# A scan and a routed expert layer in one kernel: sums, routing groups and weight loads re-timed

## The chip, the cores and the metric

The kernel runs on one core of a Trainium2 chip. Its engines are TensorE (PE in the profile, weight loads as PEld), VectorE (DVE), ScalarE (ACT), GpSimd (POOL) and SyncE (SP), which issues DMAs. Each has its own instruction stream; they wait for one another through semaphores. The metric is the time of one execution in microseconds.

## The reference, cut to what matters

The input x is 2 batches of 1024 tokens with 256 features. First comes a state-space layer: per batch 512 channels with 16 states each, `h = exp(delta*A)*h + delta*u*B` along the 1024 tokens, `y = sum over the 16 states of h*C`, then `(y + u*D) * silu(z)`, projected to 256 features by Wout and added to x. Then a layer norm, a router with 8 experts, and the experts:

```
gate_logits = x @ gate_kernel;  top 2 of 8, softmax over the two
h0 = x @ w0[e];  h1 = x @ w1[e];  inter = silu(h0) * h1        # 256 -> 512
out = sum over the two experts of weight * (inter @ wo[e])     # 512 -> 256
x = x + gb * out
```

All is float32.

## The kernel before, in words

**Scan stage.** The channels of the two batches make 8 chunks (batch times 4) of 128 partitions and 1024 tokens. Per chunk and state k of 16: TensorE spreads B into PSUM (`front`, L646), VectorE multiplies it into a drive (L1326; for states 2, 6, 10 and 14 ScalarE copies and GpSimd multiplies, L1034 and L1654), ScalarE makes the decay (L1028), VectorE scans (L1338), GpSimd multiplies with C (L1630, `weigh`), and TensorE adds the product to the chunk's sum in PSUM by an identity matmul (`back`, L664; the first of a chunk begins with u*D, L659). TensorE issues the spread of state k+4 at step k and then the sum of step k. In the last three chunks other work of TensorE takes the place of the sums in the first four steps (`pieces` of `blocks_behind`): outward matmuls of batch 0's tokens (`outward_y`), then turning of its normed tokens (`turned_in`, L701). The sums lag and are caught up, two at every other step. GpSimd may be at most six products ahead of the sums. With the last three sums go the logits of batch 0 in three pieces (`first_logits`, L720), and turning back the first two pairs of tiles (`turned_back`, L710) stands before the last sum. The ranks of batch 0 (`ranks`, L811) come after all that.

**Routing.** A token's row goes, with its position and weights, to a region of a scratch tensor in DRAM for each of its two experts. `pick`, `weights` and `place_of` on VectorE find the top two, the softmax and the destination; GpSimd sends the rows by indirect DMA, 128 rows each (`send`, L1677). The work goes in groups of token tiles, `GROUPS`: batch 0 (8 tiles, 16 sends), then two groups of 4 tiles (8 sends each). For batch 1 TensorE makes the outward matmuls (L686), VectorE adds and norms (`residual`, `normal_h2`), GpSimd takes the reciprocal root (`rstd_of`, L1659 and L1661) between its sends, TensorE turns and makes the logits (`scored`, L786 and L794). After the last group VectorE computes a table of which expert and which rows the later slots take (L1506 to L1532, end: semaphore `c_over`).

**Expert stage.** 39 slots of 128 rows: slots 0 to 7 are the first 128 rows of each expert, the others come from the table. SyncE loads a slot's rows (`rows_in`, L474). TensorE's order per slot is: turn the rows of the slot two ahead (L834), turn this slot's activations (L857), the hidden matmuls of the next slot (L849), the outward matmuls of this slot (L866). ScalarE copies and applies silu (L1147, L1153). VectorE: `take_inter` copies the turned activations (L1544), `noted_of` notes four numbers of a row, `gate_h` multiplies (L1539), `leave` weights the output (L1560, L1565). GpSimd adds each output into the result by an indirect DMA (L1714). There are two output buffers; `leave` of the first slots waits on `yo_free`, which GpSimd first raises after the last group's sends have landed (end of the GpSimd stream). Before slot 8 SyncE waits for `c_over`, for all sends, and for eight writes of zero rows behind the experts' rows, which ScalarE issues among its slots (`tail`, L1161; the wait is L494).

**Weights.** 512 KB per matrix, three per expert. SyncE loads the w1 of experts 4 to 6 during the last scans, all of experts 0 to 3 when the last sum is made, the others behind the row loads of slots 1 to 4. The hidden matmuls of an expert wait for the weights of its pair (0 and 1, 2 and 3, ...).

## Time and profile before

| | |
|---|---|
| median of 3 runs | 850.11 us (849.39 to 853.98) |
| profiled execution | 850.03 us, span 848.2 us |
| PE busy | 737.5 us (87%), 2292 instructions |
| DVE busy | 626.6 us (74%) |
| POOL busy | 513.4 us (61%) |
| ACT busy | 340.2 us (40%) |
| HBM | 98.08 MB read, 24.69 MB written |
| chain that ended last | PE 30%, of it L849 16% and L866 8% |
| queue q8, instructions | 12 packets, 0.20 MB |

The profile is of one execution. Busy times are those of an engine's instructions. The chain of waits is followed back from the last instruction to what released each step. The strip of 40 slices, each 21.2 us, shows the stages (busy tenths):

```
PE   5799998888797887878989878986699999999994
DVE  4478889999899998999999898846444444444442
POOL 1013233999999999999999898947522222222222
PEclk9999999999999999999999987997599999999998
```

### The profile page before, as it was taken

To read this page: it belongs to the slowest core of one execution; us is meant where nothing else is said; L and a number is where in the kernel's file an instruction comes from. 1 tells how busy PE (TensorE), PEld (TensorE's weight loads), DVE (VectorE), ACT (ScalarE), POOL (GpSimd) and SP (SyncE) were. 2 spreads that over 40 slices of the span, in tenths; PEclk is the share of its full clock that TensorE was granted. 3 is DMA by queue.
4 is the path that set the end of the run, shared out by engine and by line. 5 is a ranking of instruction groups with operands and counts; after the bars stand their busy time and mean duration, and the time that the engine had idled before them with its cause. 6 is when DMAs were issued, how large, how long until landed. Compare 5 with 4: busy or idle time off the path is not lost. (4 is left out here: it accounts for less than half of the span.)

```text
span 848.2 us, 9598 instructions
## 1 busy us (share of the span) xinstructions
PE 737.5 (87%) x2292; PEld 370.5 (44%) x2293; DVE 626.6 (74%) x840; ACT 340.2 (40%) x387; POOL 513.4 (61%) x271
## 2 busy tenths in 40 slices
PE   5799998888797887878989878986699999999994
PEld 2444343233232332324535323465366666666663
DVE  4478889999899998999999898846444444444442
ACT  0776966456453543545445475311111111111110
POOL 1013233999999999999999898947522222222222
PEclk9999999999999999999999987997599999999998
DMA  9354645866667666676759968567662322222220
GB/s 282 98 158 148 186 158 148 205 183 175 174 158 195 176 175 181 175 188 168 207 159 238 231 138 244 143 238 244 202 203 45 49 45 34 49 46 38 46 30 0
DMA packets 62296, 126.41 MB, mean 149 GB/s; under 512 B 11898, under 2 KB 33850, under 8 KB 62140
## 3 DMA queue, kind: packets, MB, share of 16 engines
q1 hardware_dynamic: 50468, 116.12, 50.0%
q0 software_dynamic: 7152, 8.48, 5.7%
q10 hardware_dynamic: 4648, 1.48, 0.7%
q8 instruction: 12, 0.20, 0.1%
q14 instruction: 16, 0.13, 0.1%
HBM read 98.08 MB, written 24.69 MB: 145 GB/s over the span
## 5 line engine op out<-in xcount | busy, mean ns | idle before, releaser
L1630 POOL TENSOR_TENSOR pool<-pool,hT 128x1024 f32<-128x1024 f32 x101 | 235.8, 2355 | 15.8 <-PE PS L664 15.8
L664 PE MATMUL PS<-pool,ident 128*128 128x512 f32 x404 | 206.3, 637 | 31.0 <-POOL pool L1630 30.2
L1028 ACT ACTIVATE PS<-pool,negA 128x1024 f32<-128x1024 f32 x128 | 143.1, 1118 | 168.3 <-DVE pool L1338 168.3
L1714 POOL DMA_INDIRECT out<-uT,ptab x39 | 60.6, 1555 | 169.1 <-DVE uT L1565 157.9
L1338 DVE TENSOR_TENSOR_SCAN pool<-PS,pool 128x1024 f32<-128x1024 f32 x64 | 143.0, 2270 | 3.4 <-ACT PS L1028 3.4
L849 PE MATMUL PS<-pool,uT 128*128 (+1 forms) x312 | 145.3, 610 | 0.0
L664 PEld LDWEIGHTS PS<-pool,ident 128*128 128x128 f32 x404 | 75.8, 198 | 118.4 <-issue 59.3
L646 PE MATMUL PS<-pool 96*128 96x512 bf16 x256 | 80.8, 398 | 27.9 <-DVE wz_sb L1326 12.0
L1539 DVE TENSOR_TENSOR uT<-uT,PS 128x512 f32<-128x512 f32 x39 | 26.9, 689 | 88.4 <-PE PS L849 85.6
L1654 POOL TENSOR_TENSOR spread<-spread,pool 128x1024 f32<-128x1024 f32 x32 | 75.4, 2355 | 15.3 <-ACT spread L1034 15.3
L849 PEld LDWEIGHTS PS<-pool,uT 128*128 128x128 f32 x312 | 58.3, 197 | 59.0 <-issue 59.0
L1326 DVE TENSOR_TENSOR pool<-PS,pool 128x1024 f32<-128x1024 f32 x64 | 76.9, 1202 | 8.9 <-PE PS L646 8.9
L1338 DVE TENSOR_TENSOR_SCAN pool<-PS,spread 128x1024 f32<-128x1024 f32 x32 | 73.0, 2282 | 8.2 <-POOL spread L1654 6.4
L866 PE MATMUL PS<-Y,uT 128*128 (+1 forms) x312 | 73.8, 379 | 0.9 <-DVE uT L1544 0.9
L1338 DVE TENSOR_TENSOR_SCAN pool<-PS,wz_sb 128x1024 f32<-128x1024 f32 x32 | 72.9, 2277 | 0.0
L646 PEld LDWEIGHTS PS<-pool 96*128 96x128 bf16 x256 | 22.0, 101 | 112.8 <-DVE pool L1326 35.5
L866 PEld LDWEIGHTS PS<-Y,uT 128*128 128x128 f32 x312 | 59.2, 190 | 25.3 <-issue 19.3
L1630 POOL TENSOR_TENSOR Y<-pool,hT 128x1024 f32<-128x1024 f32 x27 | 63.2, 2356 | 3.5 <-PE PS L664 3.5
L1147 ACT ACTIVATE uT<-PS 128x256 f32<-128x256 f32 x39 | 15.0, 385 | 121.1 <-PE PS L834 121.1
L664 PE MATMUL PS<-Y,ident 128*128 128x512 f32 x108 | 53.2, 622 | 1.8 <-POOL Y L1630 1.3
L559 PE MATMUL PS<-hT,pool 128*128 x112 | 50.6, 598 | 3.1 <-DVE Y L1281 2.4
L1153 ACT ACTIVATE uT<-PS 128x512 f32<-128x512 f32 x39 | 23.3, 598 | 74.3 <-PE PS L849 72.5
(197 smaller groups left out, 867.3 us busy)
## 6 DMA issues: line engine op xcount, KB each, us to landing
hT<-C_scratch SPq DMA_DIRECT2D x128, 512.0 KB, 5.3
pool<-in_w SPq DMA_DIRECT2D x16, 512.0 KB
uT<-expert_in_scratch SPq DMA_DIRECT2D x39, 130.5 KB
Y<-Y SPq DMA_DIRECT2D x32, 128.0 KB, 2.4
C_scratch<-Y SPq DMA_DIRECT2D x8, 512.0 KB, 2.6
pool<-du_scratch SPq DMA_DIRECT2D x8, 512.0 KB, 6.1
Y<-in_wo SPq DMA_DIRECT2D x8, 512.0 KB
expert_in_scratch<-zrow SPq DMA_DIRECT2D x16, 130.5 KB, 5.8
```

Source lines behind the costliest of these rows:

```text
L559: m = pe.matmul(PS[:, bank + half, :], w(k), rhs(k, half), start=k == 0, stop=k == k_chunks - 1)
L646: m = pe.matmul(PS[:, 4 + half, :], sel[0:PARTS * 32, k, :], stk[0:PARTS * 32, r, HF * half:HF * half + HF], start=True, stop=True)
L664: m = pe.matmul(PS[:, 6 + half, :], ident[:, :], prod_k[:, HF * half:HF * half + HF], start=False, stop=k == DS - 1)
L849: m = pe.matmul(PS[:, bank, :], xgT[:, r, k, :], w[:, bass.ds(e, 1), k, :].rearrange("p e n -> p (e n)"), start=k == 0, stop=k == KD - 1)
L866: m = pe.matmul(PS[:, 6 + r, 0:DM], intT[:, r, k, :], wo_sb[:, bass.ds(e, 1), k, :].rearrange("p e n -> p (e n)"), start=k == 0, stop=k == ...
L1028: act.activation(pair(2 * (k % 2)).unsqueeze(1), delta[:, chunk_at(g2, r), :], ACT.Exp, scale=decay[:, bass.ds(g2 * (2 * DS) + n, 1)]).the ...
L1326: dve.tensor_tensor(dbu_of[owned_to(k) % 3], pair(4), du[:, r, :], ALU.mult).then_inc(dbu_done, 1)
L1338: dve.tensor_tensor_scan(hst[:, k % HR, :], pair(2 * (k % 2)), driven, 0.0, ALU.mult, ALU.add).then_inc(scan_done, 1)
L1539: dve.tensor_tensor(inter[:, r, :], sil[:, r, :], PS[:, 3 + 2 * r, :], ALU.mult).then_inc(inter_done, 1)
L1630: gp.tensor_tensor(to, hst[:, k % HR, :], crep[k % RC], ALU.mult).then_inc(prod_done, 1)
L1654: gp.tensor_tensor(spread[:, :], spread[:, :], du[:, r, :], ALU.mult).then_inc(shared_done, 1)
L1714: gp.indirect_dma_start(out=out, out_offset=bass.IndirectOffsetOnAxis(ap=ptab[:, slot:slot + 1], axis=0), in_=yo[:, slot % 2, :], in_offse ...
```

## The change

Six edits. (1) The lagging sums: a table `CATCH_UP` says at which steps two are made, and the four `turned_in` go as two pairs in the first two steps of the last chunk, so that its sums begin at step 2 and not 4; ScalarE takes them as two pairs too. (2) The logits of batch 0 are one piece before sum 12; its ranks stand before sum 14, and all turning back stands behind the last sum, ScalarE's copies of it behind the copy of the sums. (3) Batch 1 is one group of 8 tiles with 16 sends, picked after both halves are normed. (4) GpSimd's sends of batch 0 are cut 10, 5, 1 around the two `rstd_of` instead of 7, 6, 3. (5) The table is cut in three parts, which VectorE computes after the outputs of slots 0, 1 and 2; the zero rows move from ScalarE's iterations 0 to 3 to 2 to 5. (6) Weights: expert 0 at the last sum, experts 1 and 2 with the first six outward tiles of batch 1, the others behind the row loads of slots 2 to 6.

```diff
-GROUPS = ((0, NTB), (NTB, NTB + TQ), (NTB + TQ, NT))
+GROUPS = ((0, NTB), (NTB, NT))
@@ SyncE
-            for e in range(CH):
-                w0_of(e)
-                w1_of(e)
-                wo_of(e)
-            sp.wait_ge(gated, NG)
-            x2_stored(slice(NTB, NTB + TQ))
+            w0_of(0)
+            w1_of(0)
+            wo_of(0)
+            for t in range(NTB, NT):
+                sp.wait_ge(o_mm, t + 1)
+                if t - NTB < 6:
+                    (w0_of, w1_of, wo_of)[(t - NTB) % 3](1 + (t - NTB) // 3)
+                if t == NTB + 6:
+                    x2_stored(slice(NTB, NTB + TQ))
...
-                if e in (1, 2, 3, 4):
-                    w0_of(e + 3)
-                    if e == 4:
-                        w1_of(e + 3)
-                    wo_of(e + 3)
+                if 2 <= e < NE - 1:
+                    w0_of(e + 1)
+                    if e + 1 < CH or e + 1 == NE - 1:
+                        w1_of(e + 1)
+                    wo_of(e + 1)
@@ TensorE
+            CATCH_UP = {0: (), 2: (4, 6), TQ: (6, 8, 10, 11)}
...
             def blocks_behind(g2, r, pieces, last):
-                made = 0
+                made, behind = 0, len(pieces)
+                sums_at = [0] * behind + [1] * (DS - behind)
+                for k in CATCH_UP[behind]:
+                    sums_at[k] += 1
                 for k in range(DS):
                     next_front(g2, r, k, last)
-                    if k < len(pieces):
-                        pieces[k]()
-                        continue
-                    for _ in range(min(2 - (k - len(pieces)) % 2, k + 1 - made)):
-                        if last and made >= DS - 3:
-                            first_logits(range(3 * (made - DS + 3), min(3 * (made - DS + 3) + 3, NTB)))
-                        if last and made == DS - 1:
-                            turned_back(0)
-                            turned_back(1)
+                    if k < behind:
+                        pieces[k]()
+                    if last and k == DS - LAG:
+                        first_logits()
+                    for _ in range(sums_at[k]):
                         if made == 0:
                             pair_read(2 * g2 + r)
+                        if last and made == DS - 2:
+                            ranks(0)
                         back(g2, r, made, prod_at(DS * (2 * g2 + r) + made))
                         made += 1
...
-            blocks_behind(NB + 1, 1, [lambda j=j: turned_in(j) for j in range(NTB // 2)], True)
-            turned_back(2)
-            turned_back(3)
+            blocks_behind(NB + 1, 1, [lambda i=i: turned_pair(i) for i in range(2)], True)
+            for j in range(NTB // 2):
+                turned_back(j)
...
-            ranks(0)
@@ ScalarE
-                if g == CH + 3 and k in range(LAG, LAG + NTB // 2):
-                    take_turned(k - LAG)
+                if g == CH + 3 and k in (LAG, LAG + 1):
+                    take_turned(2 * (k - LAG))
+                    take_turned(2 * (k - LAG) + 1)
...
-            take_rows2(0)
-            take_rows2(1)
             gap_exp(0)
             leave(NG // 2 - 1, 1)
-            take_rows2(2)
-            take_rows2(3)
+            for j in range(NTB // 2):
+                take_rows2(j)
...
-            act.wait_ge(known, 2)
-            for s2 in range(2):
+            for s2 in range(NE // 2):
                 for r in range(2):
                     take_rows(s2 + 1, r)
                     silu_h(s2 + r, 1 - r)
-                    tail(4 * s2 + 2 * r)
-                    tail(4 * s2 + 2 * r + 1)
+                    if s2 in (1, 2):
+                        if s2 == 1 and r == 0:
+                            act.wait_ge(known, 2)
+                        tail(4 * (s2 - 1) + 2 * r)
+                        tail(4 * (s2 - 1) + 2 * r + 1)
@@ VectorE
-            residual(1)
-            normal_h2(1)
-            residual(2)
+            residual(NTB, NTB + TQ)
+            normal_h2(NTB, NTB + TQ)
+            residual(NTB + TQ, NT)
+            normal_h2(NTB + TQ, NT)
             pick(1)
             weights(1)
             place_of(1)
-            normal_h2(2)
-            pick(2)
-            weights(2)
-            place_of(2)
...
-            dve.wait_ge(c_over, 1)
             dve.wait_ge(regated, 1)
...
+            def slots_of(s2, between):
                 for r in range(2):
                     take_inter(s2, r)
                     noted_of(s2 + 1, r)
                     gate_h(s2 + r, 1 - r)
                     leave(s2, r)
+                    if between:
+                        between.pop(0)()
+
+            between = [count_slots, expert_of_slots, rows_of_slots]
+            slots_of(0, between)
+            slots_of(1, between)
@@ GpSimd
-            send(0, slice(0, 7))
+            send(0, slice(0, 10))
             rstd_of(2)
-            send(0, slice(7, 13))
+            send(0, slice(10, 15))
             rstd_of(3)
-            send(0, slice(13, 16))
+            send(0, slice(15, 16))
...
             for q in range(1, NQ):
                 gp.wait_ge(placed, q + 1)
-                send(q, slice(0, 2 * TQ))
+                send(q, slice(0, 2 * NTB))
```

`count_slots`, `expert_of_slots` and `rows_of_slots` hold the instructions of the old table, L1508 to L1532, in their order. `turned_pair(i)` calls `turned_in(2 * i)` and `turned_in(2 * i + 1)`.

## Rows read from the trace of the kernel before

**Rows 1.** Busy PE, PEld, DVE, ACT, POOL by stretch; clock, DMA, GB/s.
```profile
610.20:619.00 8.80, 8.76 (x22) 5.22 (x23) 2.23 (x7) 0.98 (x2) 0.80 (x1) 0.66 1.02 355
...
619.00:833.70 214.70, 214.70 (x812) 134.53 (x811) 100.03 (x292) 36.01 (x73) 57.54 (x37) 1.00 0.28 51
```

**Rows 2.** The chain that ended last: start us, duration us, what.
```profile
558.06 1.10 PE PS L811 x44
...
585.93 2.59 DMA expert_in_scratch<-pool,posu
...
607.25 2.95 DMA uT<-expert_in_scratch
...
611.78 5.67 PE PS L849 x8
...
617.45 1.73 PE PS L866 x8
...
619.83 3.44 PE PS L849 x8
...
623.27 1.73 PE PS L866 x8
```

**Rows 3.** TensorE in order of time: start, duration, line, operation, count, idle before.
```profile
516.65 3.78 PE L659 MATMUL PS<-uT,ident 128*128 128x512 f32 x4 [0.43 <-ACT uT L1095]
...
555.30 1.88 PE L664 MATMUL PS<-pool,ident 128*128 128x512 f32 x4
```

**Rows 4.** The same view of VectorE and GpSimd, last chunk.
```profile
522.46 2.34 POOL L1630 TENSOR_TENSOR Y<-pool,hT 128x1024 f32<-128x1024 f32 x1 [3.55 <-PE PS L664]
...
524.47 1.23 DVE L1326 TENSOR_TENSOR pool<-PS,pool 128x1024 f32<-128x1024 f32 x1 [3.83 <-PE PS L646]
...
547.87 4.64 POOL L1630 TENSOR_TENSOR pool<-pool,hT 128x1024 f32<-128x1024 f32 x2
```

**Rows 5.** The same view of ScalarE and TensorE after the sums.
```profile
558.23 1.08 ACT L1100 ACTIVATE pool<-PS 128x512 f32<-128x512 f32 x2
...
562.12 15.45 PE L686 MATMUL PS<-wout_sb,uT 128*128 128x256 f32 x64 [2.97 <-DVE uT L1471]
```

**Rows 6.** The same view of GpSimd, the sends.
```profile
561.64 1.43 POOL L1677 DMA_INDIRECT expert_in_scratch<-pool,posu  x1 [8.81 <-DVEq L1467]
...
572.65 1.13 POOL L1661 TENSOR_TENSOR rstd<-rstd,nhalf 128x4 f32<-128x4 f32 x1
...
600.95 0.96 POOL L1677 DMA_INDIRECT expert_in_scratch<-pool,posu  x1 [2.63 <-DVEq L1467]
...
610.03 0.96 POOL L1677 DMA_INDIRECT expert_in_scratch<-pool,posu  x1 [0.30 <-issue]
```

**Rows 7.** The same view of VectorE, the router.
```profile
554.58 0.22 DVE L1411 COPY spread<-PS 128x64 f32<-128x64 f32 x1 [5.86 <-PE PS L720]
...
557.14 0.23 DVE L1425 TENSOR_TENSOR spread<-spread 128x64 bf16<-128x64 f32 x1
...
588.99 1.67 DVE L1402 SCALAR_TENSOR_TENSOR pool<-hT,rstd,grow 128x256 f32<-128x256 f32 x4
...
594.94 0.19 DVE L1411 COPY spread<-PS 128x32 f32<-128x32 f32 x1 [4.29 <-PE PS L794]
...
599.59 0.19 DVE L1452 TENSOR_TENSOR spread<-PS,e_rows 128x32 f32<-128x32 f32 x1 [1.80 <-remote]
```

**Rows 8.** The same view of VectorE, first output of the slots.
```profile
619.38 0.48 DVE L1565 SCALAR_TENSOR_TENSOR uT<-PS,wtab,uT 128x256 f32<-128x256 f32 x1 [0.81 <-DVE uT L1560]
```

**Rows 9.** The same view of TensorE, ScalarE, SyncE; and the wait of L494.
```profile
630.65 0.38 PE L834 MATMUL PS<-ident,uT 128*128 128x128 f32 x2
...
633.90 1.54 ACTq L1161 DMA_DIRECT2D expert_in_scratch<-zrow  x2
...
L494 SPq EVENT_SEMAPHORE  x1: 4061/4061/4061, 633.7 to 633.7; - x1
...
638.96 17.47 SPq L474 DMA_DIRECT2D uT<-expert_in_scratch  x4
```

More of the change, by code:

```diff
@@ L722, in first_logits, with ranks @@
                     m.then_inc(g_mm, 1)
+            def ranks(q):
+                first, end = GROUPS[q]
+                n = end - first
+                pe.wait_ge(tables, 1)
+                pe.wait_ge(picked, q + 1)
+                for i in range(n + (q in (0, NQ - 1))):
+                    to = PS[:, r_bank(q), P + NE * i:P + NE * i + NE]
+                    parts = [(ones[:, :], ohs[:, first + j, :]) for j in range(i)]
+                    if q:
+                        parts.append((ones[:, :], sums[:, q, :]))
+                    if i < n:
+                        parts.append((tri[:, :], ohs[:, first + i, :]))
+                    for j, (w, rhs) in enumerate(parts):
+                        m = pe.matmul(to, w, rhs, start=j == 0, stop=j == len(parts) - 1)
+                m.then_inc(rank_mm, 1)
             def next_front(g2, r, k, last):
@@ L796, in logits @@
                 m.then_inc(g_mm, 1)
-            def ranks(q):
-                first, end = GROUPS[q]
-                n = end - first
-                pe.wait_ge(tables, 1)
-                pe.wait_ge(picked, q + 1)
-                for i in range(n + (q in (0, NQ - 1))):
-                    to = PS[:, r_bank(q), P + NE * i:P + NE * i + NE]
-                    parts = [(ones[:, :], ohs[:, first + j, :]) for j in range(i)]
-                    if q:
-                        parts.append((ones[:, :], sums[:, q, :]))
-                    if i < n:
-                        parts.append((tri[:, :], ohs[:, first + i, :]))
-                    for j, (w, rhs) in enumerate(parts):
-                        m = pe.matmul(to, w, rhs, start=j == 0, stop=j == len(parts) - 1)
-                m.then_inc(rank_mm, 1)
             def scored(q):
@@ L1471, in gate_y, with residual @@
                 dve.tensor_tensor(uT[:, c, :], uT[:, c, :], szT[:, c, :], ALU.mult).then_inc(gated, 1)
-            def residual(q):
-                first, end = GROUPS[q]
+            def residual(first, end):
                 added_y(first)
@@ L1481, in residual, with normal_h2 @@
                     gathered(t)
-            def normal_h2(q):
-                for t in range(*GROUPS[q]):
+            def normal_h2(first, end):
+                for t in range(first, end):
                     centre(t)
-                for t in range(*GROUPS[q]):
+                for t in range(first, end):
                     h2_of(t)
@@ L1575, in _ @@
             gate_h(0, 0)
-            with dve.Fori(0, SPAIRS) as s2:
+            def slots_of(s2, between):
                 for r in range(2):
```

76 lines of the change are left out of this document (42 added, 34 removed).

## The prediction

> **What bounds the kernel now.** I read the page's strip of 40 slices first (PE at 9 of 10 from slice 32 on), then the chain of waits, and from there each engine in order of time. Three stages follow one another. From 620 us on a slot of the expert layer costs the same 5.82 us each time (617.45 to 623.27 in [rows 2]), TensorE is busy 214.70 of 214.70 us at a granted clock of 1.00, its 2.4 GHz level [rows 1]; half clock below is its 1.2 GHz level, and 39 slots end near 834 us. An edit moves the end only by moving the start of this stream or by opening a gap in it. Before it the scans end, GpSimd finishes its products at 552.5 [rows 4], TensorE its sums at 557.2 [rows 3]. Between them lies routing (557 to 600), a chain through all engines.
>
> Below, iteration j of the expert stream means: turn the rows of slot j+2, turn slot j's activations, hidden matmuls of slot j+1, outward matmuls of slot j. Iteration 0 starts at 610.24, iteration 3 at 630.65 [rows 9].
>
> **Sums of the last chunk.** Before, the first sum waits for ScalarE's copies of the turned tiles, starts at 516.65 at half clock [rows 3], and is done with its identity matmul when GpSimd resumes (522.46, after 3.55 us idle) and VectorE gets its next drive (524.47, after 3.83) [rows 4]. Now both pairs of tiles are turned in steps 0 and 1 and the first sum stands at step 2, ahead of two spreads of B that used to precede it. The ACT copies end near 513.6, so the first sum ends near 519.1, but VectorE's drive of state 7 is behind it and the scan that GpSimd's product 6 needs ends near 523.1. GpSimd has no gap after that before and is the bound to product 15, so its end moves +0.7, last product 553.2. Bounds: if TensorE stays at half clock through the first sum +2.2; if it runs at full clock throughout -1.5. I take +0.7, because the rows around it show half clock. The other re-timed sums (steps 6, 8, 10, 11) trade one 0.46 us stall for another: 0.
>
> The logits now go in one piece before sum 12, while GpSimd is still multiplying, and the router of batch 0 on VectorE starts when the last scan ends (about 550) instead of 554.58 [rows 7]. Ranks stand before sum 14. The tables are free early, but the last sum still waits for product 15: 555.30 + 1.8 becomes about 557.5 at its end. Turning back all four pairs (16 transposes, 1.8 us) now follows it, and ScalarE copies them after the sum's own copy. Four halves of 0.54 [rows 5] behind a 1.0 us copy end at 561.1, where before they ended at 559.3. The outward matmuls, which also waited for the gate that stood behind the router on VectorE, start at 561.2 instead of 562.12 [rows 5]: -0.9. The sends wait for the same copies: 561.6, as before (561.64) [rows 6].
>
> **Batch 1 as one group.** A send costs 1.30 us (600.95 to 610.03 is seven steps [rows 6]). Ten sends (13.1) put the first rstd at 574.7, where before it had to wait for its data until 572.2; its two operations [rows 6] end at 576.4. Five sends (6.6) and the second rstd (1.5) end at 584.6. The last four h2 rows follow at 584.8; before, the like group began at 588.99 and its last logits were read at 594.94 [rows 7], 5.9 us later. So 590.7. Picking eight tiles takes 2.8 to 2.9 (554.58 to 557.37 [rows 7]), against 1.9 for four. The ranks are 9*8/2 + 9 + 8 = 53 matmuls against 44 in 1.10 us at full clock [rows 2]; at half clock I take 1.9 (bounds 1.3 and 2.2). Places 1.3. So the places of batch 1 are known at 596.8, against 600.6 before: -3.8. I cost the 1.80 us that VectorE sat until a "remote" release at 599.59 [rows 7] at nothing in the new kernel, since the DMA engines are quiet then: weights of expert 3 and up are asked for only with slot 2.
> The Trainium skill (Runtime: NRT & Kernel Launch, section Instruction fetch mechanics) says that each sequencer refills its instructions in 16 KiB blocks by its own DMA, mostly hidden; the page's queue q8 with 12 packets and 0.20 MB agrees on the size, and the wait beside full DMA slices does not agree on "hidden". If such a refill still costs 1.8 us here, everything below is 1.8 later.
>
> **Into the slots.** The tables of later slots (VectorE 600.9 to 605) leave the path; slot 0's first turn comes at 595.7, its hidden matmuls at 597.3 (before 600.61), and the 3.4 us that TensorE waited for slot 2's rows (released by a 2.95 us transfer [rows 2] that had been issued behind the tables) go. Iteration 0 would end near 609.7 where before it ended at 619.0. The tables cost 1.2, 1.3 and 1.6 us behind the outputs of slots 0, 1 and 2, where VectorE has some 2.7 us before its next copy is missed: 0. The weights are 1.5 MB for expert 3 between slots 2 and 3, and at the 355 GB/s of [rows 1] they take 4.4 us, within one slot, while slot 2 is not multiplied before iteration 1: 0.
>
> **What is late next: the output buffers.** VectorE's output of slot 0 waits for a semaphore that GpSimd raises only behind all sends of batch 1. Before, eight sends stood behind the last places: 600.95 to 611.0, plus 1.6 us to landing (585.93 + 2.59 against an issue of 0.96 [rows 2, 6]), 612.6, and the output at 619.38 waited for nothing but its own engine [rows 8]. Now sixteen stand there. Placed at 596.8, first send at 597.2, last issued at 597.2 + 15*1.31 + 0.96 = 617.8, landed 619.4. The output of slot 0 is wanted at 609.7 and gets 619.5 to 620.0; behind it on VectorE stand the count of the slots (1.2) and the copy of slot 1's activations (0.7), so slot 1's outward matmuls start at 622.0. TensorE has then idled since about 613.5. Before, those matmuls started at 623.27 [rows 2]: -1.3. But they now start behind an idle time. Before, TensorE restarted at 610.24 after 3.4 us idle, and to 617.45 took 7.2 us for what costs 4.3 later (5.67 against 3.44 for the same eight matmuls [rows 2]): 2.9 us at half clock. The other such restart, 562.12, cost 1.7. I take 2.9: from iteration 2 on the stream stands at **+1.6**. Bounds -2.5 (places and sends 3 us earlier, restart at 1.7) to +4.5.
>
> **The tails, moved two iterations back.** ScalarE writes zero rows behind each expert's rows, two per iteration, formerly in iterations 0 to 3, now in 2 to 5. SyncE may load slot 8 only when all eight have landed. Before, iteration 3 started at 630.65, the last pair was issued from 633.90, SyncE's wait for them lasted 4.06 us from 633.7 to 637.8, and slot 8's load was issued at 638.96 [rows 9]. With 2.3 to 2.95 us to landing ([rows 2], a busier moment) its rows are there at 641.8, 11.2 us after the start of that iteration. That load is not used before iteration 6, so it cost nothing. Now the last pair is in iteration 5, its rows come 11.2 us after that starts, and TensorE wants them as the first thing of iteration 6, 5.82 after: a gap of **5.4 us** (4.6 to 6.5). Everything on TensorE stands behind that turn. The restart costs another 2.2 (between the two rows, 1.7 and 2.9). Slot 9's load is issued right after slot 8's, so the gap comes once.
> The Trainium skill (DMA: Bandwidth & Descriptors, section Anatomy of one DMA) fits a transfer as 2.0 us plus its bytes at 436 GB/s; 130.5 KB would be 2.3 us, near the short end of what I read for the load, and with it the gap would be 4.9.
>
> **Sum.** Stream +1.6, gap +5.4, restart +2.2: +9.2 on a span of 848.2. The profiled execution took 850.03, 1.8 more than its span, and stands at the median (850.11). So 859.2.
>
> **Rivals.**
> (a) *Only the buffers are late.* If slot 8's rows come in time, the stream's +1.6 is all: 851.7. For it: SyncE has slack everywhere else. Against it: the wait of 4.06 us is in the trace already, and only its three spare iterations hid it.
> (b) *Neither is late, faster.* The stream starts when slot 2's rows allow, 9.3 us earlier, ends 9.3 earlier: 840.8. It needs the 16 sends to be done before 609, when slot 0's output is wanted; it decides where sends plus landing take less than 12 us. Against it: 1.30 us each.
> (c) *Only the gap at slot 8.* -9.3 + 5.4 + 2.2 = -1.7: 848.3. It needs the same early sends.
> (d) *The scans starve.* TensorE at half clock through the last chunk keeps VectorE waiting for its drives and the sends start 3 us later; everything hangs on the sends, so 862.2, and to 866 where a refill is added.
> The spreading of the weights may not do what it says: at six of the steps SyncE waits for outward tiles that come every 1.7 us, as fast as 512 KB arrive, so the DMA engines stay as full as before until 577. That changes no term.
>
> **How the numbers follow.** Forecast 0.62; (a) 0.13; (b) 0.08; (c) 0.05; (d) 0.12. The forecast's own range is 853 to 864. For 8 in 10 I go from 850.5 to 864.5, which takes in (a) and most of (d). About 0.5% (4.3 us) is what a measurement of this kernel can tell from no change. Slower (over 854.4): 0.57 of the forecast and (d), together 0.69. Same: (a), (c) and the forecast's low end, 0.21. Faster: (b) and what is left, 0.10.
>
> **What would show it.** In the new trace: the first output of VectorE in the slots released by GpSimd's last sends, not by TensorE, near 619.5; TensorE idle some 8 us in iteration 1 before slot 1's outward matmuls, at half clock behind it; SyncE waiting several us for the zero rows after slot 7's load; TensorE idle about 5 us, once, before the turn of slot 8, near 649; and 5.82 us a slot afterwards. The forecast is wrong if the first output comes before 612, if slot 8's turn has no idle time before it, or if the places of batch 1 come later than 600.

## The result, and the profile after

The changed kernel took 864.89 us, median of 4 runs (857.29 to 866.55); the kernel before, beside it, 849.75, median of 4 (847.76 to 853.98). The ratio is 1.0154, 95% interval 1.0081 to 1.0227: slower, by somewhere between 0.8 and 2.3%. Run again on another chip it was 1.0145 (1.0098 to 1.0192). The profiled execution took 863.47 with a span of 861.7, 13.5 us more than the span before. The forecast was 859.2, so the direction was right. The profiled 863.47 lies in the forecast's own range (853 to 864), the median is 0.9 us above it and 0.4 above the range for 8 in 10. Of the 5.7 us between forecast and median, 4.3 are in the profiled execution and are to be explained; the other 1.4 are the distance of the median from it.

I follow the time from the front. VectorE in the last two chunks (start us, duration, what, and the idle time before it with its releaser):

```profile
495.41 1.22 DVE L1336 TENSOR_TENSOR pool<-PS,pool 128x1024 f32<-128x1024 f32 x1 [1.69 <-PE PS L651]
...
522.21 1.23 DVE L1336 TENSOR_TENSOR wz_sb<-PS,pool 128x1024 f32<-128x1024 f32 x1 [5.76 <-PE PS L651]
```

The second row answers to the 3.83 us of [rows 4]; the prediction had this drive behind the first sum and put +0.7 us on it for GpSimd. The first has no answer there: in the chunk before the last, where the plan of the sums has two at a time at steps 10 and 11, VectorE now waits for the spread of B, which TensorE makes behind them. TensorE, from step 11 of that chunk to the outward matmuls:

```profile
489.72 5.16 PE L669 MATMUL PS<-Y,ident 128*128 128x512 f32 x8
...
516.09 3.78 PE L664 MATMUL PS<-uT,ident 128*128 128x512 f32 x4 [2.94 <-ACT uT L1104]
...
548.02 4.53 PE L724 MATMUL PS<-gate_sb,uT 128*128 128x8 f32 x32 [0.63 <-DVE wz_sb L1336]
552.41 6.25 PE L669 MATMUL PS<-Y,ident 128*128 128x512 f32 x8
...
559.60 3.68 PE L669 MATMUL PS<-pool,ident 128*128 128x512 f32 x8
563.11 1.91 PE L715 MATMUL PS<-ident,uT 128*128 128x128 f32 x16
566.48 3.69 PE L691 MATMUL PS<-wout_sb,uT 128*128 128x256 f32 x16 [1.46 <-ACT pool L1109]
```

GpSimd's last product ends at 555.85. Before it ended at 552.5 and the last sum ran at 555.30 [rows 3, 4], behind two other pieces of TensorE's:

```profile
553.59 0.95 PE L720 MATMUL PS<-gate_sb,uT 128*128 128x8 f32 x8
554.40 1.07 PE L710 MATMUL PS<-ident,uT 128*128 128x128 f32 x8
```

Here the logits are one block of 4.53 us and the two sums behind it take 6.25 for x8 (3.68 for the like x8 at 559.60). TensorE is busy all the time, but at the 1.2 GHz level for about 6 us. By stretches, columns as in [rows 1], the changed kernel and then the kernel before:

```profile
551.00:557.00 6.00, 6.00 (x14) 3.42 (x14) 5.50 (x31) 0.21 (x1) 5.23 (x5) 0.50 0.01 1
```
```profile
550.00:553.00 3.00, 3.00 (x17) 2.10 (x16) 0.00 (x0) 0.00 (x0) 2.83 (x4) 1.00 0.00 0
```

What TensorE did before the clock fell were the 32 narrow matmuls of the logits (8 columns each) in one piece. All six traces that have them in one piece show the fall, for about 3 to 6 us; in the eight that have them in three pieces between sums the granted clock stays at 1.00 there. Then come the ranks, from 558.49 on, right behind the two sums, and two sums are still to do when they end. The last sum ends at 563.1, 7.2 us behind the last product; before it was 4.7.

GpSimd's sends of batch 1, its first row and its last, and the add into the output behind them:

```profile
602.71 1.06 POOL L1696 DMA_INDIRECT expert_in_scratch<-pool,posu  x1 [11.09 <-DVEq L1477]
...
621.83 0.96 POOL L1696 DMA_INDIRECT expert_in_scratch<-pool,posu  x1 [0.30 <-issue]
626.89 1.62 POOL L1733 DMA_INDIRECT out<-uT,ptab  x1 [4.10 <-DVE uT L1576]
```

Sixteen steps of 1.27 us, one behind the other, where [rows 6] had eight. The chain of waits runs through all sixteen, then through their landing:

```profile
621.83 3.50 DMA expert_in_scratch<-pool,posu
625.60 0.48 DVE uT L1576
627.04 0.70 DVE uT L1555
627.78 3.78 PE PS L875 x8
```

VectorE and TensorE there; the row of VectorE answers to [rows 8], where it waited for nothing but its own engine:

```profile
625.60 0.48 DVE L1576 SCALAR_TENSOR_TENSOR uT<-PS,wtab,uT 128x256 f32<-128x256 f32 x1 [11.99 <-POOLq L1727]
```
```profile
627.78 3.78 PE L875 MATMUL PS<-Y,uT 128*128 128x256 f32 x8 [7.19 <-DVE uT L1555]
```

The releaser is GpSimd's queue at L1727, the raise of the buffers' semaphore behind the sends. The outward matmuls take 3.78 for what takes 1.73 at the other clock level. The last gap, in the chain and in the view of TensorE:

```profile
652.71 0.34 ACTq L1169
...
653.83 2.63 DMA expert_in_scratch<-zrow
657.71 2.04 DMA uT<-expert_in_scratch
659.80 0.55 PE PS L843 x2
...
661.21 4.58 PE PS L858 x8
...
668.18 3.44 PE PS L858 x8
```
```profile
659.80 0.55 PE L843 MATMUL PS<-ident,uT 128*128 128x128 f32 x2 [4.36 <-DMA uT<-expert_in_scratch]
```

SyncE's longest wait for the zero rows (in total us, times, longest), 4.06 before in [rows 9]:

```profile
SPq L497 <- DMA expert_in_scratch<-zrow: 14.3, 1, 14.3
```

By stretches of 10 us, columns as in [rows 1], granted clock after the busy times:

```profile
610.00:620.00 10.00, 7.87 (x27) 4.33 (x26) 1.18 (x4) 0.94 (x2) 7.56 (x9) 1.00 1.04 356
620.00:630.00 10.00, 2.81 (x7) 1.85 (x6) 3.33 (x14) 0.64 (x2) 3.80 (x4) 0.79 0.46 141
630.00:640.00 10.00, 10.00 (x36) 6.63 (x35) 5.42 (x16) 1.37 (x3) 2.12 (x2) 0.87 0.84 234
640.00:650.00 10.00, 10.00 (x40) 6.42 (x39) 5.06 (x16) 1.70 (x4) 2.56 (x2) 1.00 0.68 191
650.00:660.00 10.00, 5.64 (x21) 3.17 (x20) 3.02 (x9) 0.86 (x2) 3.09 (x2) 1.00 0.33 63
660.00:670.00 10.00, 10.00 (x33) 6.04 (x32) 3.88 (x13) 1.44 (x4) 0.92 (x1) 0.83 0.12 32
```

TensorE loses 7.2 us in the second stretch and 4.4 in the fifth, and has the lower clock behind each. Hidden matmuls of iteration 2 begin at 632.6 against 625.5 before: +7.1. Those of iteration 7 begin at 668.18 against 654.74: +13.4, which is the whole difference of the spans. So 7.1 to 7.2 come from the start of the stream and 6.25 from slot 8.

### The profile page after: what moved, and what is told of

The parts are those of the page before. It is cut to its first block and busy times, and to the rows that moved or that the text cites. A ratio compares the mean times of both kernels' runs of the same rounds, so it can differ in the third digit from the quotient of the medians.

```text
span 861.7 us, 9562 instructions
## 1 busy us (share of the span) xinstructions
PE 738.7 (86%) x2312; PEld 371.3 (43%) x2313; DVE 624.0 (72%) x824; ACT 340.0 (39%) x386; POOL 512.6 (59%) x271
## 5 line engine op out<-in xcount | busy, mean ns | idle before, releaser
L1733 POOL DMA_INDIRECT out<-uT,ptab x39 | 60.6, 1555 | 170.8 <-DVE uT L1576 159.7
L858 PE MATMUL PS<-pool,uT 128*128 (+1 forms) x312 | 143.0, 602 | 0.0
L651 PE MATMUL PS<-pool 96*128 96x512 bf16 x256 | 78.4, 388 | 33.6 <-DVE pool L1336 15.4
L875 PE MATMUL PS<-Y,uT 128*128 (+1 forms) x312 | 75.7, 386 | 8.1 <-DVE uT L1555 8.1
```

What stands on the lines that cost most here:

```text
L651: m = pe.matmul(PS[:, 4 + half, :], sel[0:PARTS * 32, k, :], stk[0:PARTS * 32, r, HF * half:HF * half + HF], start=True, stop=True)
L858: m = pe.matmul(PS[:, bank, :], xgT[:, r, k, :], w[:, bass.ds(e, 1), k, :].rearrange("p e n -> p (e n)"), start=k == 0, stop=k == KD - 1)
L875: m = pe.matmul(PS[:, 6 + r, 0:DM], intT[:, r, k, :], wo_sb[:, bass.ds(e, 1), k, :].rearrange("p e n -> p (e n)"), start=k == 0, stop=k == ...
L1733: gp.indirect_dma_start(out=out, out_offset=bass.IndirectOffsetOnAxis(ap=ptab[:, slot:slot + 1], axis=0), in_=yo[:, slot % 2, :], in_offse ...
```

## The experiments

Beside the first two, the kernels ran in four sets, each on a chip of its own and at a time of its own, and the kernel before beside each. Its median there was 842.42 (set A), 849.09 (B), 844.76 (C) and 848.16 (D). The scans differ by up to 6 us between traces, so each kernel has two numbers: its ratio within its set, and, from its trace, the time **from the last product to the end** of the span. All in us; P: last product ends; then from P to the first send, to the end of the last send's issue, to the end of the span; then the waits of VectorE behind 540 us whose releaser the profile calls "remote", of which more below:

```
kernel                  set  median  ratio  [95%]             P       send  sends  end    "remote"
before                  -    849.75  -                        552.45   9.2   58.5  295.8  3.73, 1.80
before, again           D    847.72  1.000  [0.997, 1.003]    549.23   9.2   60.7  296.8  3.83, 1.82
changed                 -    864.89  1.0154 [1.0081, 1.0227]  555.85  11.6   64.4  305.9  -
changed, again          B    862.00  1.0145 [1.0098, 1.0192]  553.09  11.6   66.9  305.1  4.17
e1 zero rows 4 + 4      A    854.18  1.0117 [1.0070, 1.0165]  553.27  11.6   66.8  299.1  -
e2 buffers early        A    860.30  1.0191 [1.0133, 1.0250]  553.14  11.6   66.3  305.6  -
e3 three groups         A    850.99  1.0093 [1.0060, 1.0126]  553.11   9.9   55.0  295.6  -
e4 old logits           B    858.72  1.0105 [1.0076, 1.0135]  554.12   9.2   64.7  302.3  -
e5 old plan and logits  A    853.60  1.0131 [1.0076, 1.0187]  548.67   9.2   64.7  302.5  -
e6 before, tails late   B    854.50  1.0066 [1.0038, 1.0093]  550.97   9.2   58.7  300.1  3.8, 1.8
a2 changed, old weights C    865.26  1.0216 [1.0168, 1.0264]  558.52  11.6   61.8  305.0  -
c1 combined             B    845.01  0.9951 [0.9922, 0.9979]  554.59   9.2   60.6  293.9  1.89, 4.06
c1 combined, again      C    841.98  0.9968 [0.9939, 0.9996]  548.84   9.2   54.7  288.0  -
c2 combined, old weights C   843.85  0.9970 [0.9941, 0.9999]  554.30   9.2   54.6  288.1  -
```

**The two late things, each alone.** e1 takes the changed kernel and issues the zero rows four at a time in iterations 2 and 3, so that the last land two iterations earlier:

```diff
-                    if s2 in (1, 2):
-                        if s2 == 1 and r == 0:
+                    if s2 == 1:
+                        if r == 0:
                             act.wait_ge(known, 2)
-                        tail(4 * (s2 - 1) + 2 * r)
-                        tail(4 * (s2 - 1) + 2 * r + 1)
+                        for e in range(4 * r, 4 * r + 4):
+                            tail(e)
```

> The changed kernel with one edit: ScalarE issues its eight zero-row writes in iterations 2 and 3, four in each, and not two in each of iterations 2 to 5. My theory: the 4.4 us that TensorE idles before the turn of slot 8, and the restart at half clock behind it (together 6.2 us in the changed kernel), come from the last of these writes. Then both go: 6.2 us faster than the changed kernel (864.9), about 858.7. A rival (slot 8's rows are late for another reason, the later table or the sends that must have landed): no change, 864.9.

VectorE's wait for the buffers stays, 11.21 us (TensorE waits 8.3), and the gap at slot 8 is gone: the hidden matmuls of iterations 5 and 6 start at 647.2 and 653.0, 5.8 apart. From the last product to the end it is 299.1, 6.0 less than the changed kernel's own second trace (305.1) and 6.8 less than its first, as the theory said. By the ratios alone (1.0117 against 1.0145 and 1.0154) it would be 2 to 3 us; the last experiments tell why ratios of different sets don't compare. The row of VectorE:

```profile
622.24 0.48 DVE L1576 SCALAR_TENSOR_TENSOR uT<-PS,wtab,uT 128x256 f32<-128x256 f32 x1 [11.21 <-POOLq L1727]
```

e6 does the reverse: the kernel before, with nothing but its zero rows in iterations 2 to 5.

```diff
-            act.wait_ge(known, 2)
-            for s2 in range(2):
+            for s2 in range(NE // 2):
                 for r in range(2):
                     take_rows(s2 + 1, r)
                     silu_h(s2 + r, 1 - r)
-                    tail(4 * s2 + 2 * r)
-                    tail(4 * s2 + 2 * r + 1)
+                    if s2 in (1, 2):
+                        if s2 == 1 and r == 0:
+                            act.wait_ge(known, 2)
+                        tail(4 * (s2 - 1) + 2 * r)
+                        tail(4 * (s2 - 1) + 2 * r + 1)
```

> The kernel before with one edit: ScalarE's zero rows two iterations later, as in the change. My theory: TensorE idles 4.4 us before the turn of slot 8 and restarts at half clock: 6.2 us slower than before, ratio 1.0074. A rival (the gap in the change needs its other edits, the later weight loads above all): no change, 1.000.

```profile
649.38 0.69 PE L834 MATMUL PS<-ident,uT 128*128 128x128 f32 x2 [4.17 <-DMA uT<-expert_in_scratch]
```

1.0066 (1.0038 to 1.0093), and the gap is there, alone in a kernel that had none. The hidden matmuls around it are 10.8 us apart (639.9, 650.7) where 5.8 is the rule: 5.0 at that step, and 0.9 at the next, which runs in part at the lower clock. Both directions agree: the late zero rows cost about 6 us (6.25 in the changed kernel, 6.0 to 6.8 gained in e1, 5.9 here, 5.6 by e6's ratio). From the last product on e6 is only 3.3 to 4.3 us longer than the kernel before, whose first output came 1.6 to 2.5 us later than e6's.

e2 raises the semaphore of the output buffers before the sends of batch 1 instead of behind them:

```diff
             gp.wait_ge(noted, 4)
+            gp.sem_inc(yo_free, 2)
             for q in range(1, NQ):
...
             gp.wait_ge(x2_out, 16 * 3)
-            gp.sem_inc(yo_free, 2)
```

> The changed kernel with one edit: GpSimd gives the two output buffers free before the sends of batch 1 and not behind their landing; the adds into the result still stand behind them. My theory: VectorE's first output waits for the 16 sends. Then outputs 0 and 1 come in time, output 2 waits for the first add, due near 630, within its slack: iteration 3 starts near 628 and not at 637.8, 9.8 us faster, about 855. A rival (the stream starts late because TensorE restarts at half clock and the weights of expert 3 are asked for late, and the buffers are hidden by that): no change to 2 us, 863 to 865.

The promised 9.8 us did not come: 1.0191, 305.6 us behind the last product, as much as the changed kernel. The outputs of slots 0 and 1 are in time now (619.59, idle 0.62). But slot 2's output needs the first buffer back, and this is how GpSimd, VectorE and TensorE stand in that trace:

```profile
624.83 1.62 POOL L1733 DMA_INDIRECT out<-uT,ptab  x1 [5.36 <-DMA expert_in_scratch<-pool,posu]
634.13 1.57 POOL L1733 DMA_INDIRECT out<-uT,ptab  x1 [7.68 <-DVE uT L1576]
```
```profile
619.59 0.48 DVE L1576 SCALAR_TENSOR_TENSOR uT<-PS,wtab,uT 128x256 f32<-128x256 f32 x1 [0.62 <-DVE uT L1571]
633.43 0.48 DVE L1576 SCALAR_TENSOR_TENSOR uT<-PS,wtab,uT 128x256 f32<-128x256 f32 x1 [8.67 <-POOLq L1732]
```

The add of slot 0 stands behind the same sixteen sends and their landing on GpSimd, is issued at 624.83 and is over only when VectorE is released at 633.4. The wait moved one turn on with its length. So the semaphore was the place of the wait, not its cause; the cause is GpSimd's queue, which is taken by the sends until 619.5 in that trace and, with their landing, until 624.8.

**Group of eight or two groups of four.** e3 keeps the whole change but cuts its second group into two again:

```diff
-GROUPS = ((0, NTB), (NTB, NT))
+GROUPS = ((0, NTB), (NTB, NTB + TQ), (NTB + TQ, NT))
...
+            pick(2)
+            weights(2)
+            place_of(2)
...
-                send(q, slice(0, 2 * NTB))
+                send(q, slice(0, 2 * TQ))
```

> The changed kernel with one edit: batch 1 is again two groups of four tiles, each picked, placed and sent by itself. My theory: eight sends and not sixteen stand behind the last places, which come at the same time as now (near 602, because the router of the first group goes in between on VectorE); the buffers are free near 615 and the first output is wanted near 614. Then the wait and the restart behind it go: 9 to 10 us faster, about 855. A rival (the one group brought the places of batch 1 earlier and that is worth more than the sends cost): slower than the changed kernel, by 2 to 4 us.

```profile
607.17 0.96 POOL L1699 DMA_INDIRECT expert_in_scratch<-pool,posu  x1 [0.30 <-issue]
615.37 1.62 POOL L1736 DMA_INDIRECT out<-uT,ptab  x1 [7.24 <-DVE uT L1579]
```
```profile
646.22 0.69 PE L843 MATMUL PS<-ident,uT 128*128 128x128 f32 x2 [4.69 <-DMA uT<-expert_in_scratch]
```

The last send is over 55.0 us behind the last product, not 64 to 67: eight of the sixteen are issued while VectorE and TensorE still work on the last four tiles. TensorE has no wait above 0.5 us left before the outputs of slots 1 and 2 (hidden matmuls at 605.9, 612.4, 618.8, 624.6), the gap at slot 8 stays. It is 295.6 against 305.1, and against 305.6 of e2 on the same chip: 9.5 to 10 us less, as the theory said. But 1.7 of them are not the group's. The first send comes 9.9 us behind the last product and not 11.6, in a stage that this edit doesn't touch: in this trace the clock behind the logits was down for 3 us and not 6, and the two sums took 5.12 us and not 6.25. The one group itself costs about 8 us.

**The end of the scans.** e4 gives back the logits in three pieces, the ranks behind the sums and the turning back around the last sum, and keeps the new plan of the sums. e5 gives back the plan too. The core of both:

```diff
-                    if last and k == DS - LAG:
-                        first_logits()
...
+                        if last and made >= DS - 3:
+                            first_logits(range(3 * (made - DS + 3), min(3 * (made - DS + 3) + 3, NTB)))
+                        if last and made == DS - 1:
+                            turned_back(0)
+                            turned_back(1)
```
```diff
-                sums_at = [0] * behind + [1] * (DS - behind)
-                for k in CATCH_UP[behind]:
-                    sums_at[k] += 1
+                sums_at = [0 if k < behind else 2 - (k - behind) % 2 for k in range(DS)]
```

> The changed kernel with the logits of batch 0 in three pieces again, its ranks behind the last sum and the turning back and its copies in the old order; the new steps of the sums stay. My theory: logits and ranks ahead of the last sums cost 2.4 us of the 5.9 us by which the last sum was late, and the order of the copies 1 us more at the sends; the rest is the new steps. Then 3 us faster than the changed kernel (ratio to before 1.0115). A rival (the new steps of the sums are all of it): no change, 1.015.

> The changed kernel with the scan stage's end as before: old steps of the lagging sums and of turning the tiles, logits in three pieces, ranks behind the last sum, turning back and its copies in the old order; one group, tables, zero rows and weights as in the change. My theory: the last product came 3.4 us and the last sum 5.9 us later than before, and the sends start 5.8 us later; all of the stream stands behind the sends. Then it is 5 to 6 us faster than the changed kernel, about 859.4. A rival (these parts lie beside other work, and the sends' start is set by something else): within 1 us of the changed kernel.

e4 came out as its theory had it: 1.0105 beside 1.0145 for the change in the same set, and 302.3 against 305.1 from the last product on. The first send comes 9.2 us behind the last product in both, as before, against 11.6: the new order of logits, ranks and turning back costs 2.4, and 0.7 in e3, where the lower clock was shorter. What the plan costs is in front of the last product. I count the last 21 operations over 128x1024 of GpSimd, about a chunk, and the 21 before them. The 21 before took 56.14 to 56.30 us in all seven traces with the new plan and 54.34 to 54.39 in all seven with the old: +1.8, with a stall of VectorE of 1.69 to 1.83 (the one at 495.41) in each of the first seven and in none of the others. The last 21 took 53.65 to 54.34 against 52.24 to 52.93: +1.3. e5's sends run from 557.87; everything behind is as late relative to them as in the change, and both waits are still there:

```profile
557.87 1.43 POOL L1698 DMA_INDIRECT expert_in_scratch<-pool,posu  x1 [8.83 <-DVEq L1479]
```

So the plan costs 3.1 us and the order of the logits 2.4, together 5.5, within e5's theory of 5 to 6. By its ratio, 1.0131, it would be 1 to 2 us, but the change itself was not run in set A. The ratios of e5 (set A) and e4 (set B) can't be set against each other, for a reason that the last experiments gave.

**The change again**, for a second trace:

> The changed kernel itself, on the chip of the next three. Both theories: 1.015 times the kernel before, with TensorE's two idle times before slot 1's outward matmuls (7 to 8 us) and before the turn of slot 8 (4.4 us).

Both waits are there again, 7.40 and 4.07 us, and 305.1 us from the last product to the end against 305.9.

**A combination.** c1 takes from the change the tables between the slots, the weights spread and the split of the sends of batch 0; it has three groups, the old end of the scans, and the zero rows 4 + 4. Its edits are those of e1, e3 and e5 in one.

> The changed kernel with the scan stage's end as before, batch 1 in two groups again, and the zero rows four and four in iterations 2 and 3; of the change there stay the tables between the slots and the spread weights. My theory: no idle time on TensorE in the stream, which starts 5 us earlier than before since the tables are off its path: ratio 0.994. A rival (the tables between the slots or the weights loaded late cost what they save): 1.000 or slower.

0.9951 (0.9922 to 0.9979), then 0.9968 (0.9939 to 0.9996) on another chip: faster than both kernels, 0.3 to 0.5% faster than the kernel before. TensorE's one wait above 1 us in the slots is 2.34 us at 619.21 in the first trace; the second has none. c2 is c1 with the weights asked for as before, and a2 is the change with the same edit (behind the slots' row loads, too, the weights come as before, which is not shown here):

```diff
-            w0_of(0)
-            w1_of(0)
-            wo_of(0)
-            for t in range(NTB, NT):
-                sp.wait_ge(o_mm, t + 1)
-                if t - NTB < 6:
-                    (w0_of, w1_of, wo_of)[(t - NTB) % 3](1 + (t - NTB) // 3)
-                if t == NTB + 6:
-                    x2_stored(slice(NTB, NTB + TQ))
+            for e in range(CH):
+                w0_of(e)
+                w1_of(e)
+                wo_of(e)
+            sp.wait_ge(gated, NG)
+            x2_stored(slice(NTB, NTB + TQ))
```

> This is the combined kernel with the weight loads of the kernel before (experts 0 to 2 asked for at once after the gates of slice NG - 1, then from slot 1 on those of experts 4 to 7): against the kernel before, only the tables between slots, the zero rows 4 + 4 in the third pair and the split of the sends differ. Theory A, the spread of the weights costs: in the combined kernel slot 3's rows queued behind 1.5 MB of expert 3's weights (turn of that slot waited 2.34 us at 619.21) and VectorE waited 4.06 us for its instructions at 616.88; both go, and the ratio falls from 0.9951 to about 0.991 (some 3 us less). Rival B, the spread keeps the transfers of the sends short: then the first adds and the sends of the second and third batch end later, the outputs of slots 0 to 2 come late, and the ratio is 0.997 or more. No effect: 0.995.

> The combined kernel once more, beside its copy with the old weight loads on the same chip: 0.995 again if its gain is real (its first comparison had 7 runs), 1.000 if that was the chip.

> The changed kernel with the weight loads of the kernel before. Both late waits (7.2 to 7.4 us at the fourth product of the outputs, 4.1 us ahead of the turn of slot 8) are set by batch 1's sends and by the eight zero rows, not by the weights: theory, ratio 1.013 to 1.0145, as the changed kernel's. If the full queues of 614 to 623 us (weights of experts 1 to 3 beside the sends) had held up the last sends' landing, the first wait would fall from 7.4 to about 4 us and the ratio to 1.009. If instead the early weights collide with the sends of batch 0, the start comes later and the ratio is 1.017.

c2 and c1 are alike on one chip, 288.1 and 288.0 behind the last product, 0.9970 and 0.9968: theory A, that the spread costs 3 us, falls, and its rival with it. What I had taken for its price stood in c1's first trace, in set B, beside two waits of VectorE:

```profile
604.00 0.19 DVE L1464 TENSOR_TENSOR spread<-PS,e_rows 128x32 f32<-128x32 f32 x1 [1.89 <-remote]
...
616.88 0.69 DVE L1555 TENSOR_TENSOR uT<-uT,PS 128x512 f32<-128x512 f32 x1 [4.06 <-remote]
```

Neither is in c1's second trace, which is 5.9 us shorter behind the last product. The two add up to 5.95, but that is chance. The sends of the first trace are over 5.9 us later already (60.6 against 54.7), at 615.2, ahead of the second wait, and the first output of the slots waits for them in both. The time was lost in the routing: the ranks of batch 1's first group start 34.9 us behind the last product against 30.7, behind a wait of ScalarE that the profile calls "remote" too, and the 1.89 comes on top. ScalarE in c1's first trace and in its second, where it waits for TensorE alone and starts 25.6 us behind the last product, not 27.6:

```profile
582.14 0.66 ACT L1135 ACTIVATE hT<-PS 128x256 f32<-128x256 f32 x2 [20.69 <-remote]
```
```profile
574.42 0.66 ACT L1135 ACTIVATE hT<-PS 128x256 f32<-128x256 f32 x2 [18.71 <-PE PS L812]
```

The granted clock over the logits behind it was 0.69 (582.5 to 587.4), and 1.00 over those of the second trace (574.8 to 578.0).

Two results still did not fit: a2 at 1.0216, above all that was expected of it, and c2, 7.7 us shorter behind the last product than the kernel before but only 0.3% faster. Was 295.8 one long execution?

> The kernel before, unchanged, once more, for a second trace. From the last product to the end it took 295.8 us in its first trace (848.2 - 552.45), its copy with the tables between the slots and the zero rows 4 + 4 took 288.1, a difference of 7.7, while their times differ by 0.3% (2.5 us). If the 295.8 is the rule, the second trace shows 295 to 297 and the small difference of the times is made before that stretch (the scans, 4 to 6 us apart from trace to trace). If the first trace was a long one, the second shows 289 to 292. Ratio 1.000 either way.

It was not: 296.8, with two "remote" waits at the same places. In sets A and C no trace has such a wait (seven traces, on any engine); in B and D and in the first two traces every one has some, on VectorE or ScalarE. The kernel before takes 842.4 and 844.8 in A and C, 848.2 and 849.1 in D and B. Its two waits end idle times of 5.5 to 5.7 us together, both on VectorE in the routing, ahead of the places of batch 1's two groups. Its sends are over 58.5 to 60.7 us behind P (58.7 in e6), c2's at 54.6; c2 also splits the sends of batch 0 otherwise, so not all of these 3.9 to 6.1 us need be the waits.

If the waits are missing in A and C, the kernel before needs about 290.6 there (c2's 288.1 and 0.3% of 844.76; an estimate, no trace of it was taken in these sets). In the change they fall beside its sixteen sends (e1 in A and the change in B have their sends over 66.8 and 66.9 behind P), so that it gains nothing where they are missing. The ratios can be estimated from this, with 3.1 for the plan in front of P. In A and C: a2 305.0 - 290.6 + 3.1 = 17.5, or 1.021 for 1.0216; e3 8.1, 1.010 for 1.0093; e2 18.1, 1.0215 for 1.0191; e1 11.6, 1.014 for 1.0117; e5, with the old plan, 11.9, 1.014 for 1.0131. In B, with 296.3 for the kernel before (the mean of its two traces, neither from B): the change 11.9, 1.014 for 1.0145; e4 9.1, 1.0107 for 1.0105; e6 3.8, 1.0045 for 1.0066; c1 -2.4, 0.997 for 0.9951. All lie within the measured intervals. So a2 need be no slower than the change: from the last product to the end it took 305.0 with the old weights, the change 305.1 and 305.9. And the change would be slower by about 2% on a chip where the kernel before has no such waits; it wasn't run on one.

Why the scans of one plan end at 549 in some executions and at 554 in others none of these runs tells.

## Why the prediction was right, and by how much it was off

**Places of batch 1 and the sends.** Mechanism right, all of it late. Forecast and measured: last sum ends 557.5, 563.1; first send 561.6, 567.43; first send of batch 1 597.2, 602.71; last one over 617.8, 622.8; landed 619.4, 625.3; first output 619.5 to 620.0, 625.60; slot 1's outward matmuls 622.0, 627.78. The 5.8 us at the end are there at the first send already. From there to the first send of batch 1 it is 35.3 us for a forecast 35.6. Still, one of the prediction's own signs of being wrong is met: the places of batch 1 came at 601.9, later than 600.

The step that failed is "Sums of the last chunk" with its end. Its first part is the products, +0.7 forecast, but +3.1 over the old plan measured, of which 1.8 is the stall in the chunk before the last. The failed sentence is "the other re-timed sums (steps 6, 8, 10, 11) trade one 0.46 us stall for another: 0". Its second part is what comes behind the last product: 4.3 us to the end of the last sum in the forecast, 7.2 measured. The clause "the last sum still waits for product 15: 555.30 + 1.8" misread [rows 3, 4]: product 15 was done at 552.5, and the last sum waited 2.8 us for TensorE's own other pieces. In the new kernel, when product 15 came (555.85), TensorE had sums 13 and 14 and the ranks still before it, because the logits stood ahead of sum 12 in one block and the clock behind them was half as high (0.58 granted from 552.4 to 558.6, where the kernel before had 1.00). The ranks waited for nobody: VectorE's pick was done at 556.6, they ran at 558.49 behind the sums, and took 1.1 us. The prediction had no term for the clock here.

**The output buffers** were the next thing late, with the releaser named, TensorE idle 7.2 us (forecast about 8) and the lower clock behind it. e3 shows the cause by taking it away: the wait at slot 1 goes with the one group. e2 shows that my wording "waits for a semaphore" was too narrow: freeing the buffers alone gives nothing, since the adds stand in the same queue.

**The zero rows.** Gap forecast 5.4, measured 4.36; restart forecast 2.2, measured 1.9; together 7.6 forecast, 6.25 measured. The rows of slot 8 were there 10.3 us after the start of that iteration (649.46 to 659.75) and not 11.2. The last pair was issued 3.25 us into it, as before (652.71 here, 633.90 against 630.65 in [rows 9]); what was shorter is the load, 2.04 us, where I allowed up to 2.95 from a busier moment. The Trainium skill (DMA: Bandwidth & Descriptors, section Anatomy of one DMA) has a fit for DMAs that GpSimd issues; SyncE issues this load. Taken over as an estimate it gives 2.3, and the 2.04 measured is nearer to it than to my 2.95.

**Weights and tables cost nothing** held: c1 and c2 are alike, and no gap is theirs. **No "remote" wait of VectorE on the path** held in the first trace; in the second there is one of 4.17 at 611.44, ahead of the wait for the buffers, which hides it.

In sum: start +7.2 for +1.6, slot 8 +6.25 for +7.6, together 13.45 for 9.2. Two errors of opposite sign, 5.6 and 1.35, partly cancel in the time; that is luck. Rival (a), only the buffers late, is e1, 1.0117 where 851.7 would be 1.002: what it leaves out is the late start. Rival (c), only the gap, is e3, and its price was too low: 1.0093 for no change, since the plan's 3.1 us and the later first send are in it. Rival (b), neither late and faster, is c1: right in sign, but 0.3 to 0.5% for the 1.1% that it promised. Part of the 9.3 us that I counted as free in the kernel before, its 1.80 us among them, is there only on some chips. Rival (d), the scans starve, was half right, and its 862.2 is nearer to the profiled 863.47 than the forecast is: 3.1 us came from the scans, 1.3 in the last chunk as it said and 1.8 by the double sums a chunk earlier; the backlog and the clock at the end of the sums added most of the rest.

## What to carry to other kernels

When work is merged into one larger group, ask which queue holds the items that the small groups had spread out, and what else stands behind them in that queue; freeing the semaphore there does not help if the consumer's own DMA stands in the same queue. When a step is moved later because it has slack, count the slack in the unit of the loop it feeds. A block put ahead of an in-order engine's last pieces makes them late if they come out just as it runs, and here TensorE's clock fell behind the block too (0.7 to 2.4 us more to the first send in all): leave small gaps filled with small pieces. Two waits that add up to a difference are not yet its cause: count events from a common point and see where the difference first stands.

## What the runs showed of the hardware

- TensorE's granted clock fell from 1.00 to 0.50 while the profile has the engine busy, during or right behind 32 matmuls of 8 columns in one piece, in six traces of six (0.50 from 551 to 557 in the changed kernel); with the same matmuls in three pieces between sums of 512 columns it stayed at 1.00 in eight of eight, e4 among them, which up to there differs from the change in the place of the logits alone. The eight matmuls of two sums took 6.25 us behind the fall and 3.68 at 1.00.
- Waits that the profile puts down to "remote" went with the set, which is one chip at one time: none in seven traces of two sets, some in each of the seven others, and the kernel before 3.4 to 6.7 us slower in the sets that had them. In the changed kernel ScalarE had the longest:

```profile
619.66 0.39 ACT L1155 ACTIVATE uT<-PS 128x256 f32<-128x256 f32 x1 [8.31 <-remote]
625.32 0.60 ACT L1161 ACTIVATE uT<-PS 128x512 f32<-128x512 f32 x1 [5.28 <-remote]
```

  The times in brackets are the engine's whole idle time, and the "remote" release is only its end: the transposes that the first of these copies ran at 616.3 to 616.7, so at most 2.9 of the 8.31 us are its. They cost nothing there, beside TensorE's own wait: a2, with none, took as long from the last product on. The first lies where the DMA share is 1.04 (610 to 620). The Trainium skill (Runtime: NRT & Kernel Launch, section Instruction fetch mechanics) says that engines refill their instructions by DMA, mostly hidden. These waits fit a refill that queues behind data, and where they stand in the routing they are not hidden (c1's two traces are 5.9 us apart, with the lower clock behind such a wait in it); that they are refills was not tested, nor why one set should have them and another not.
- The same kind of indirect DMA was over 2.59 us after its start in [rows 2] and 3.50 in the last send here. With the DMA share at 0.93 (620 to 630 us in e2) the add issued at 624.83 released its buffer at about 633.4, 8.5 us later.
- TensorE ran the same eight outward matmuls in 3.78 us after 7.19 us idle, at a granted clock half as high (the 1.2 GHz level), and in 1.73 at the 2.4 GHz level; it was back at a clock of 1.00 in the stretch from 640.
